# Expert stage of a graph layer: the low halves of the token rows come through two transposing DMAs a block

## The reference

```python
x = x + gnn(layernorm(x)) + attention(layernorm(x))     # 6250 nodes x 256
t = layernorm(x)
top, idx = top_k(t @ Wg + bg + bias, 2)                  # 2 of 8 experts
w = softmax(top)
x = x + sum over the two experts e of w_e * (relu(t @ W1[e] + b1[e]) @ W2[e] + b2[e])   # 256 -> 512 -> 256
```

## Time and profile before

| | |
|---|---|
| median of 3 runs | 2488.24 us (2487.57 to 2488.42) |
| profiled execution, its own time | 2485.35 us |
| its span in the profile | 2483.8 us |
| granted clock of TensorE, mean over the span | 0.92 |
| TensorE busy | 2174.1 us, 88% of the span |
| VectorE, ScalarE, GpSimd busy | 1599.2, 1182.6, 372.5 us |
| matmuls of up (L2179) and of down (L2194) | 1344 each, 157 us each |
| transposes of the blocks (L2161) | 448 |
| loads of blocks (`big<-rows_dram`) | 56 of 265.0 KB |
| scatters to the output (L874) | 112 |

### The profile page before, as it was taken

How to read it: one execution, slowest core, us unless ns; L and a number is a source line. 1 busy time by engine, 2 the same in 40 slices (tenths; PEclk the granted TensorE clock), 3 DMA queues, 4 the chain that set the end, 5 groups by cost and what they waited for, 6 DMA issues and landing times.

```text
span 2483.8 us, 52951 instructions
## 1 busy us (share of the span) xinstructions
PE 2174.1 (88%) x15108; PEld 1344.1 (54%) x15109; DVE 1599.2 (64%) x4787; ACT 1182.6 (48%) x2382; POOL 372.5 (15%) x431
## 2 busy tenths in 40 slices
PE   2555656599999999999899998999999999499997
PEld 1434444355555565565455554444444444499996
DVE  6999998688888888888332233354545445355554
ACT  2444443255555555555444444244444444366664
POOL 1000000100000000000111001112121121266665
PEclk9665566799999999999899999999999999699998
DMA  2111111022222222222212111555555554555553
GB/s 78 39 33 34 41 35 42 27 117 114 113 111 115 116 107 115 116 111 116 97 55 91 49 49 73 220 197 188 205 181 204 186 201 151 183 94 93 87 93 47
DMA packets 125655, 268.58 MB, mean 108 GB/s; under 512 B 30382, under 2 KB 79071, under 8 KB 123411
## 3 DMA queue, kind: packets, MB, share of 16 engines
q1 hardware_dynamic: 99587, 216.49, 24.6%
q0 software_dynamic: 26000, 51.27, 8.9%
HBM read 137.14 MB, written 132.41 MB: 109 GB/s over the span
## 4 chain that ended last, share of the span: by engine, by line
PE 65%; issue 15%; DVE 9%; DVEq 4%; POOLq 2%; POOL 1%; DMA 1%; SPq 1%; ACT 1%; ACTq 0%
PE bank L1982 43%; PE bank L1973 6%; PE bank L2194 6%; PE bank L2179 5%; POOLq L756 2%; DVE big L1014 2%; DVEq L1029 1%; DVE big L1004 1%; DVEq L1000 1%; DVEq L1013 1%; DVE big L1011 1%; PE bank L2161 1%; DVE R L989 1%; PE bank L1990 1%; DVE R L982 0%
## 5 line engine op out<-in xcount | busy, mean ns | idle before, releaser
L1982 PE MATMUL bank<-RW,big 128*128 128x512 f16 (+1 forms) x4900 | 1181.4, 380 | 0.0
L1982 PEld LDWEIGHTS bank<-RW,big 128*128 128x128 f16 x4900 | 444.2, 98 | 396.7 <-issue 4.4
L1672 ACT ACTIVATE big<-bank 128x512 f16<-128x512 f32 (+1 forms) x640 | 372.9, 583 | 334.6 <-PE bank L1973 334.4
L1161 DVE TENSOR_TENSOR big<-iotaB,keys 128x512 f16<-128x512 f16 x1300 | 452.7, 422 | 7.9 <-issue 7.8
L1973 PE MATMUL bank<-big 128*128 128x128 f16 x2560 | 248.5, 220 | 12.3 <-DVE big L1161 12.0
L1973 PEld LDWEIGHTS bank<-big 128*128 128x128 f16 x2560 | 191.1, 98 | 124.2 <-DVE big L1161 13.0
L874 POOL DMA_INDIRECT out_dram<-big x112 | 179.5, 1603 | 111.9 <-ACT big L1811 80.3
L1802 ACT ACTIVATE big<-bank,b1A,iscA 128x256 f32<-128x256 f32 x224 | 114.6, 562 | 103.3 <-PE bank L2179 103.0
L2194 PE MATMUL bank<-RW,big 128*128 (+1 forms) x1344 | 157.3, 274 | 0.0
L2179 PE MATMUL bank<-big,RW 128*128 128x256 f16 x1344 | 156.8, 274 | 0.4 <-ACT big L1791 0.4
L2179 PEld LDWEIGHTS bank<-big,RW 128*128 (+1 forms) x1344 | 132.0, 98 | 16.3 <-ACT big L1791 0.6
(11 more groups left out here) (377 smaller groups left out, 2858.1 us busy)
## 6 DMA issues: line engine op xcount, KB each, us to landing
big<-a_dram SPq DMA_DIRECT2D x49, 832.0 KB, 6.1
big<-a_dram SPq DMA_DIRECT2D x49, 768.0 KB, 4.5
a_dram<-big SPq DMA_DIRECT2D x49, 640.0 KB, 3.0
a_dram<-big SPq DMA_DIRECT2D x49, 512.0 KB, 2.6
a_dram<-big SPq DMA_DIRECT2D x49, 448.0 KB, 2.5
big<-rows_dram SPq DMA_DIRECT2D x56, 265.0 KB
big<-in_x_dram SPq DMA_DIRECT2D x96, 128.0 KB, 2.0
big<-in_L_ffn_W_dram POOLq DMA_DIRECT2D x16, 512.0 KB, 4.7
```

The costliest lines, as they stand in the source:

```text
L1161: last = v.tensor_tensor(out[q].rearrange("p b (m k) -> p b m k", k=2), inturn(iotaB[:, :], QB, P // 2), twice(kd[:, q * QB:(q + 1) * QB, ...
L1672: a.activation(Ab[q][:, 0:n], banks[BB(q)][:, 0:n], ACT.Copy).then_inc(s_ab, 1)
L1982: last = mm(bank[:, :], blk(q, c), src, start=(u == 0), stop=(u == T))
```

## The change

The 256 rows are loaded so that partition p gets rows p and p+128 of the block. TensorE turns only the high half (four transposes), ScalarE copies only 512 columns to `xt5[0][par]`. The low half is loaded once more, straight from the table, by two transposing DMAs on SyncE's queue into `xt5[1][par]` (two times 128 partitions x 256 columns); `up5` waits for them with a semaphore pair of its own, `s_xlow`. In `load5` they are issued after a wait for up of block b-2. At the start the pads are written after the transposing DMAs of blocks 0 and 1 have landed.

```diff
--- before.py
+++ after.py
@@ -345,10 +345,10 @@
         b2b = big[:, spo.at:spo.at + EXPERTS * D].rearrange("p (e n) -> p e n", e=EXPERTS)
         sp5 = Space()
+        xt5 = [[sp5.f16(2 * BLK).rearrange("p (c n) -> p c n", c=2) for _ in range(2)] for _ in range(2)]
         xbr = [sp5.f16(2 * ROWW) for _ in range(2)]
         xb5 = [r.rearrange("p (j n) -> p j n", j=2) for r in xbr]
         xbg = [r.bitcast(F32).rearrange("p (j n) -> p j n", j=2)[:, :, D:D + GATE] for r in xbr]
-        xt5 = [sp5.f16(4 * BLK).rearrange("p (c n) -> p c n", c=4) for _ in range(2)]
         h32 = [sp5.f32(4 * BLK) for _ in range(2)]
         hhi, hlo = ([sp5.f16(4 * BLK) for _ in range(2)] for _ in range(2))
         y5 = [sp5.f32(2 * D) for _ in range(2)]
@@ -510,6 +510,7 @@
         s_pad = sem("s_pad")
         s_b2 = sem("s_b2")
         s_xb = [sem(f"s_xb{i}") for i in range(2)]
+        s_xlow = [sem(f"s_xlow{i}") for i in range(2)]
         s_tx = sem("s_tx")
         s_xc = sem("s_xc")
         s_up = sem("s_up")
@@ -654,13 +655,21 @@
             sp.wait_ge(s_sx[1], 32 * (T // 2))
             sp.wait_ge(s_xc, 2)
             sp.wait_ge(s_we, 32)
+            def lows5(r, par):
+                for k in range(2):
+                    sp.dma_start_transpose(out=xt5[1][par][:, k, :],
+                                           in_=rows_dram.bitcast(F16)[r, D + k * P:D + (k + 1) * P])\
+                      .then_inc(s_xlow[par], 16)
+
             for e in range(2):
-                sp.dma_start(xbr[e].bitcast(F32),
-                             rows_dram[e * REG:e * REG + BLK, :].rearrange("(p j) c -> p (j c)", j=2))\
+                sp.dma_start(xbr[e].bitcast(F32).rearrange("p (j c) -> p j c", j=2),
+                             rows_dram[e * REG:e * REG + BLK, :].rearrange("(j p) c -> p j c", j=2))\
                   .then_inc(s_xb[e], 16)
+                lows5(slice(e * REG, e * REG + BLK), e)
             sp.wait_ge(s_tab, 1)
             for e in range(2):
                 sp.wait_ge(s_xb[e], 16)
+                sp.wait_ge(s_xlow[e], 32)
             for e in range(EXPERTS):
                 r = sp.value_load(padI[0:1, e:e + 1], min_val=0, max_val=SPARE_ROW - BLK)
                 sp.dma_start(rows_dram[bass.ds(r, BLK), :].rearrange("(p j) c -> p j c", j=2), zrows)\
@@ -672,9 +681,11 @@
                 n = sp.value_load(needI[0:1, bass.ds(b, 1)], min_val=16, max_val=48)
                 r = sp.value_load(rowI[0:1, bass.ds(b, 1)], min_val=0, max_val=SPARE_ROW)
                 sp.wait_ge(s_we, n)
-                sp.dma_start(xbr[par].bitcast(F32),
-                             rows_dram[bass.ds(r, BLK), :].rearrange("(p j) c -> p (j c)", j=2))\
+                sp.dma_start(xbr[par].bitcast(F32).rearrange("p (j c) -> p j c", j=2),
+                             rows_dram[bass.ds(r, BLK), :].rearrange("(j p) c -> p j c", j=2))\
                   .then_inc(s_xb[par], 16)
+                sp.wait_ge(s_up, b * 2 + 2)
+                lows5(bass.ds(r, BLK), par)
             for b in range(2, 4):
                 load5(b, b % 2)
@@ -1788,7 +1799,7 @@
                 act.wait_ge(s_tx, b + 3)
                 act.wait_ge(s_up, b * 2 + 2)
                 a.activation(gates[:, bass.ds(b * (2 * GATE), 2 * GATE)].rearrange("p (j n) -> p j n", j=2), xbg[par], ACT.Copy)
-                a.activation(xt5[par].rearrange("p c n -> p (c n)"), bankh[4 + par][:, :], ACT.Copy).then_inc(s_xc, 1)
+                a.activation(xt5[0][par].rearrange("p c n -> p (c n)"), bankh[4 + par][:, 0:2 * BLK], ACT.Copy).then_inc(s_xc, 1)
             def relu5(b, par):
                 if isinstance(b, int) and b == 2:
@@ -2156,19 +2167,20 @@
                 pe.wait_ge(s_xb[par], half * 16 + 16)
                 pe.wait_ge(s_xc, b + 1)
-                for c in range(4):
+                for c in range(2):
                     for j in range(2):
                         last = nc.tensor.transpose(bankh[4 + par][:, (2 * c + j) * P:(2 * c + j + 1) * P],
                                                    xb5[par][:, j, c * P:(c + 1) * P], ident16[:, :])
                 last.then_inc(s_tx, 1)
-            def up5(b, par):
+            def up5(b, par, half):
                 if isinstance(b, int) and b == 2:
                     pe.wait_ge(s_tab, 1)
                 e = b if isinstance(b, int) and b < 2 else \
                     pe.value_load(expI[0:1, bass.ds(b, 1)], min_val=0, max_val=EXPERTS - 1)
                 pe.wait_ge(s_xc, b + 3)
+                pe.wait_ge(s_xlow[par], half * 32 + 32)
                 for f in range(4):
                     if f % 2 == 0:
                         pe.wait_ge(s_ua, b * 2 + (f // 2 + 1))
@@ -2176,7 +2188,7 @@
                     n = 0
                     for k in range(2):
                         for wp, xp in ((0, 0), (0, 1), (1, 0)):
-                            last = mm(o, w1(e, wp, k, f), xt5[par][:, 2 * xp + k, :], start=(n == 0), stop=(n == 5))
+                            last = mm(o, w1(e, wp, k, f), xt5[xp][par][:, k, :], start=(n == 0), stop=(n == 5))
                             n += 1
                     if f % 2 == 1:
                         last.then_inc(s_up, 1)
@@ -2199,17 +2211,17 @@
             turned5(0, 0, 0)
             turned5(1, 1, 0)
-            up5(0, 0)
+            up5(0, 0, 0)
             for b in range(2):
-                up5(b + 1, 1 - b)
+                up5(b + 1, 1 - b, (b + 1) // 2)
                 turned5(b + 2, b, 1)
                 down5(b, b)
             with pe.Fori(1, NBLK // 2 - 1) as k:
                 for par in range(2):
-                    up5(2 * k + par + 1, 1 - par)
+                    up5(2 * k + par + 1, 1 - par, k + par)
                     turned5(2 * k + par + 2, par, k + 1)
                     down5(2 * k + par, par)
-            up5(NBLK - 1, 1)
+            up5(NBLK - 1, 1, NBLK // 2 - 1)
             down5(NBLK - 2, 0)
             down5(NBLK - 1, 1)
```

## The result

The changed kernel took 2494.32 us in the median of 10 runs (2489.49 to 2499.08), the kernel before 2488.51 us (2486.82 to 2492.27, 10 runs): ratio 1.0022, 95% interval 1.0011 to 1.0032. It is slower by about 5.5 us. The forecast was 2481 and faster. The profiled execution has a span of 2489.1 us against 2483.8.

The account below looks back on a forecast made before the run. TensorE was taken to bound the expert stage with a beat of 5.69 us a block. Saving 12.5 us, less 3.0 and 2.0 at the start, gave -7.5 us and 2481; the range was 2476 to 2507.

Parts of the forecast that it names:

- 1.0 taken: In the beat: two transposing DMAs assumed to take 1.0 us of all 16 DMA engines a block, TensorE staying the bound.
- 0.9 taken: On SyncE's queue: issuing one transposing DMA assumed to take 0.9 us, with room for two issues a block.
- 11.6 us that 52 blocks were to give: In the beat: four transposes fewer in blocks 3 to 54 save 52 x 0.222 = 11.6 us.
- the term (b): At the start: block 2's load, in smaller packets alternating with the weights, lands later; 2.0 us more.
- in time: At the start: block 2's low halves arrive before its up if they take one or two packets an engine; nothing charged.
- The rival with this mechanism: At block 2: low halves wait packet by packet behind weights; 2488; chance 0.24, shared with start costs that eat the gain.
- the DMA engines as the bound: In the beat: two transposing DMAs take over 2.2 us of all engines a block; 2493 to 2530; chance 0.20.
- an element a packet: In the beat: every 2 B element its own packet, 33 us; chance 0.05, shared with tiles in a row.
- the pads that wait: At the start: pads wait for the low halves of blocks 0 and 1; 3.0 us more, all on the chain.
- Tiles one behind the other: In the beat: four tiles each hold all engines 1.5 us; +190 us, 2680; chance 0.05, shared with an element a packet.
- Late scatters: In the beat: contention delays scatters over 3.6 us and TensorE stops; beat 0.5 longer costs 27, 2508; chance 0.05.

Follow-up runs that it names:

- e6: The changed kernel, but blocks 0 and 1 turned wholly on TensorE, transposing DMAs from block 2 on: 2487.92 us, ratio 1.0006 to the kernel before.
- e3: The kernel before with only the row layout changed (rows p and p+128 on partition p), no transposing DMA: 2489.97 us, ratio 1.0011.
- e1: The changed kernel, but blocks 0 to 3 turned wholly on TensorE, transposing DMAs from block 4 on: 2482.07 us, ratio 0.9977 to the kernel before.
- e8: As e1, but blocks 0 to 3 also loaded with both rows in one piece of 2120 B: 2481.94 us, ratio 0.9982 to the kernel before.
- e12: As e8, but blocks 0 to 5 loaded and turned as in the kernel before: 2481.07 us, ratio 0.9973 to the kernel before.
- e2: The changed kernel, with GpSimd issuing the 6 MB of weights only after the low halves of blocks 2 and 3 landed: 2491.79 us, ratio 1.0018.
- e10: The changed kernel with the 6 MB of weights in eight DMAs, pieces of 1 KB in the code: 2492.53 us, ratio 1.0025 to the kernel before.
- e11: As e8, but TensorE's loop body has four blocks instead of two: 2480.95 us, ratio 0.9976 to the kernel before.
- e7: As e1, but each transposing DMA issued twice, up waiting for all four: 2574.93 us, ratio 1.0351 to the kernel before.
- e4: As e1, but TensorE reads down's expert number inside up: 2487.74 us, ratio 1.0002 to the kernel before.
- e9: As e8, but TensorE reads both expert numbers ahead of up: 2490.97 us, ratio 1.0023 to the kernel before.

## Why the prediction was wrong

**The beat** was read rightly, but for one term. Four transposes cost 0.222 us on the chain and their removal shows at once; the transposing DMAs add 0.6 us of the engines a block (1.0 taken); SyncE's issue is 1.15 (0.9 taken); scatters have room; the granted clock stays full (1.00 from 2200 to 2400). What was missed is 0.12 us in every second beat, 26 x 0.12 = 3.1 us: of the 11.6 us that 52 blocks were to give, 8.2 came. Eight transposes gave TensorE's queue 0.45 us to read down's expert number and compute; four give 0.22, and once in each turn of the loop that isn't enough. I had costed the removed transposes as if TensorE's own queue were free.

**The start** is the step that failed: the term (b), 2.0 us for block 2's load and nothing for its low halves, with the sentence that these "are in time" if they take one or two packets an engine. They take 32, one for each row of 256 B, as the packets of the DMA view show, and each waits its turn behind a packet of weights (200 to 202 in 4 us). The rival with this mechanism gave up of block 2 for 2169 and it began at 2169.16; it gave the gain as just used up, and the clock and the 3.1 us made it a loss. The measured 2494 lies inside the wide range of 2476 to 2507 only because that range was stretched for another rival, the DMA engines as the bound, to which the prediction gave 2493 to 2530 and which did not come: that is luck. (One sum there is off and changes nothing: an element a packet would be 65536 x 10.6 ns / 16 = 43 us, not 33.) Of the 14.1 us up to the transposes of block 3, the starts of up of block 2 in the table separate 4.1 for the pads that wait (41.44 against 37.29 in e6; 3.0 predicted), 5.0 for the low halves (37.29 against 32.31 in e3; nothing predicted) and 3.3 for the split rows (32.31 against 29.02; 2.0 predicted). The other 1.7 are that up at the lower clock (4.46 against 2.62 on the chain).

**The other rivals.** The DMA engines as the bound in the beat did not come: 70% busy, and still not full with twice the transposing DMAs. Tiles one behind the other did not come either: four tiles a block add 0.6 us of the engines. The Trainium skill, "VectorE: DVE Perf Modes", "The three transpose paths", has 1309 ns for a tile by DMA; by these rows that isn't time in which a tile holds all engines. The 261 GB/s of the Trainium skill, "DMA: Bandwidth & Descriptors", "Latency and other measured facts", would be 0.5 us for the 128 KB of a block. The rows here give 0.6 by both queues together, about 220 GB/s, and 1.0 by the hardware queue's packets alone, 131 GB/s. Late scatters did not stop the beat.

**Whether the cause is settled.** That the loss is made at the start is shown by e1, e8 and e12, which keep the change from block 4 or 6 on and are faster than the kernel before. That it is the weights' traffic is shown by e2, where the stall moved to the block that met them. That turns are taken by packets is shown by the counts of both queues in the changed kernel, in e10 and in e2 (195 to 194 packets from 2168 to 2172), and the split rows (e3) and the smaller packets (e10) move up of block 2 by about what this gives, 3.3 us where 2.7 was worked out and 6.2 where the estimate is 6.2. That the 0.12 us come once in each turn of the loop is shown by e11; what in that turn costs TensorE's queue its lead stays open.

## What to carry to other kernels

A DMA that is hidden in the steady state must be placed once more in the start, beside the largest transfer that runs there: count its packets for each engine, not its bytes, since with a few hundred small packets beside a queue of large ones 64 KB took 15 us and more to land. When a cheap change is good for the loop and bad for the first blocks, keep the old way for the first blocks (e12_first_six: 0.9973 where the whole change was 1.0022). And work that leaves an engine was perhaps the cover for the register reads in that engine's own queue.

## What the runs showed of the hardware

- A transposing DMA of 256 rows by 128 fp16 columns from DRAM takes 1.12 to 1.24 us of SyncE's queue against 0.32 to 0.41 for a plain load; while the weights came in one issue took 5.3 us.
- It moves one packet for each row of 256 B. In the beat a pair of them adds 1.0 us of all 16 DMA engines to the hardware queue's packets and 0.6 us to those of both queues together, and a second pair 0.6 more (e7).
- While both queues have work, they take turns packet by packet, whatever the size: 200 packets of 8.2 KB to 202 of 256 B in 4 us, 336 of 3.9 KB to 339 (e10).
- Next to a software queue with 8 KB packets the second of a pair landed 15.46 us after its issue (e2). Next to one with 3.9 KB packets it was 18.62 (e10), there with block 2's load and low halves still ahead of it in its own queue.
- Pieces of 1 KB of a load issued by GpSimd went out as packets of 3.9 KB (e10).
- A load of 265 KB lands in 3.0 to 3.1 us alone, in 6.1 to 6.2 beside the weights in pieces of 2120 B, and in 9.0 to 9.4 in pieces of 1060 B.
- A read of a register's value of 0.30 us in TensorE's queue showed no cost in the beats before (one of 52 was 0.2 us longer), cost 0.12 us once in each turn of the loop with half the transposes, and 0.25 inside the up matmuls (e4); two reads together cost up to 0.54 (e9).
